# Set-up of an attention and mixture-of-experts kernel: keys in two halves, first maxima among other products, small loads on two other queues

## The reference

```python
q1 = split_heads(query @ q1_w.T); q2 = split_heads(query @ q2_w.T)      # query = layernorm(x)
k1, v1 = key @ kv1_w.T;           k2 = key @ kv2_w.T                    # key = context
attn1 = softmax(q1 k1^T * SCALE); attn2 = softmax(q2 k2^T * SCALE)
x = (attn1 - (lambda_1 - lambda_2 + 0.1) * attn2) @ v1
x = rmsnorm(x) * norm_w @ proj_w.T + proj_b                             # added to the input
probs = softmax(layernorm(x) @ gate_w.T); w, idx = top_k(probs, 2); w = w / sum(w)
out = x + sum over chosen experts of w_e * ((silu(x @ g_e.T) * (x @ u_e.T)) @ down_e.T)
```

## Time and profile before

| | us |
|---|---|
| median of 3 runs | 556.72 |
| lowest, highest run | 552.91, 558.14 |
| span of the profiled execution | 555.4 |
| PE busy, share | 495.3, 89% |
| DVE, ACT, POOL busy | 386.1, 340.2, 273.4 |

### The profile page before, as it was taken

How to read it: one execution, slowest core, us unless ns; L and a number is a source line. 1 busy time by engine, 2 the same in 40 slices (tenths; PEclk the granted TensorE clock), 3 DMA queues, 4 the chain that set the end, 5 groups by cost and what they waited for, 6 DMA issues and landing times.

```text
span 555.4 us, 12114 instructions
## 1 busy us (share of the span) xinstructions
PE 495.3 (89%) x3741; PEld 363.6 (65%) x3756; DVE 386.1 (70%) x805; ACT 340.2 (61%) x642; POOL 273.4 (49%) x347
## 2 busy tenths in 40 slices
PE   4695889998999888799798999999999999999990
PEld 3463546775666555526566888878888888777750
DVE  5437458888888765788577997887667677666551
ACT  1220588888788888374675777766656566645530
POOL 5006464574564564203227566656567555644244
PEclk9986799999999989899999999999999999999996
DMA  7567757768658632563666777967555465554224
GB/s 215 191 171 174 239 147 231 203 171 264 192 170 253 200 118 76 179 204 112 152 137 111 158 129 195 180 120 157 94 104 86 85 84 101 96 68 77 30 30 47
DMA packets 88090, 79.89 MB, mean 144 GB/s; under 512 B 49176, under 2 KB 73368, under 8 KB 87896
## 3 DMA queue, kind: packets, MB, share of 16 engines
q1 hardware_dynamic: 76512, 63.38, 41.8%
q0 software_dynamic: 11520, 15.74, 17.6%
HBM read 49.08 MB, written 22.41 MB: 129 GB/s over the span
## 4 chain that ended last, share of the span: by engine, by line
PE 67%; DVE 10%; ACT 7%; DMA 5%; issue 5%; SPq 3%; POOL 2%; another core or an unknown queue 0%; ACTq 0%; POOLq 0%
PE bank L1459 27%; PE bank L1476 13%; PE bank L1242 5%; PE bank L1288 4%; DMA x_parts<-WE 3%; PE bank L1274 3%; PE bank L1488 2%; PE bank L1256 2%; PE bank L1311 2%; PE bank L1324 2%; DVE FB L1165 2%; PE bank L1297 2%; DVE FB L1169 2%; ACT FB L876 2%; PE bank L1336 2%
## 5 line engine op out<-in xcount | busy, mean ns | idle before, releaser
L1459 PE MATMUL bank<-FB,WE 128*128 128x0 bf16 x1440 | 187.6, 280 | 2.6 <-issue 1.0
L1459 PEld LDWEIGHTS bank<-FB,WE 128*128 x1440 | 136.1, 98 | 34.9 <-issue 4.3
L709 POOL DMA_INDIRECT out<-FB,slot_tok x60 | 99.9, 1665 | 91.2 <-DVE FB L1186 85.4
L876 ACT ACTIVATE FB<-FB 128x512 bf16<-128x512 f32 x120 | 75.6, 630 | 69.9 <-DVE FB L1165 63.8
L1169 DVE TENSOR_TENSOR FB<-FB 128x512 bf16<-128x512 f32 x120 | 83.3, 694 | 46.9 <-ACT FB L876 43.0
L1476 PE MATMUL bank<-FB,WE 128*128 128x0 bf16 x720 | 103.7, 280 | 4.3 <-DVE FB L1169 2.2
L1165 DVE TENSOR_TENSOR FB<-FB,bank 128x512 f32<-128x512 f32 x120 | 81.9, 683 | 27.8 <-ACT FB L870 21.5
L700 POOL DMA_INDIRECT FB<-x_parts,slot_tok x60 | 61.7, 1028 | 68.0 <-DMA FB<-FB 26.7
L870 ACT ACTIVATE FB<-bank 128x512 f32<-128x512 f32 x120 | 70.7, 589 | 33.9 <-PE bank L1459 29.3
L1476 PEld LDWEIGHTS bank<-FB,WE 128*128 x720 | 67.6, 98 | 23.5 <-issue 7.8
L633 POOL TENSOR_TENSOR WE<-FB,WE 128x256 bf16<-128x256 f32 x104 | 67.8, 678 | 22.1 <-ACT WE L740 22.0
(11 more groups left out here) (180 smaller groups left out, 616.4 us busy)
## 6 DMA issues: line engine op xcount, KB each, us to landing
FB<-w SPq DMA_DIRECT2D x26, 512.0 KB, 5.5
WE<-w SPq DMA_DIRECT2D x44, 256.0 KB
WE<-q_parts SPq DMA_DIRECT2D x32, 200.0 KB
WE<-x SPq DMA_DIRECT2D x16, 256.0 KB, 5.2
q_parts<-FB SPq DMA_DIRECT2D x32, 128.0 KB
x_parts<-WE SPq DMA_DIRECT2D x20, 128.0 KB, 4.0
out<-WE SPq DMA_DIRECT2D x20, 128.0 KB, 5.5
q_parts<-WE SPq DMA_DIRECT2D x16, 128.0 KB
```

Source lines behind the costliest of these rows:

```text
L709: pool.indirect_dma_start(out=out, out_offset=bass.IndirectOffsetOnAxis(ap=slot_tok[:, c:c + 1].bitcast(U32), axis=0), in_=result_tile(c), ...
L876: nc.scalar.activation(hT[k % 3][:, 0, :], hid[k % 2], ACT.Copy).then_inc(hi_ready, 1)
L1459: ins = nc.tensor.matmul(to, wf[:, bass.ds(at + o, P)], xgT[s % 2][:, 2 * part + kc, :].shape_from_register(long[s % 2]), start=(z == 0), ...
```

## The change

It touches the set-up alone; the steps of the batches and the experts' stage stay as they are.

- Keys are made in two halves of four batches (308 columns each), in two sets of tiles and two tensors in device memory. The second half comes after the queries of batch 0. `scores` of batch 0 waits for all of it, `scores_for_max` only for the first.
- The 12 groups of scores for batch 0 start after two of the eight value products; the other six, the queries of batch 1 and the transposition of batch 2 stand between them.
- Queries of batch 2 come after the transposed maxima, the second half of them after the first two `scores`.
- Values are copied by ACT in place of DVE.
- ACT issues the reads of batch 0's keys (4 transfers in place of 8) behind a wait for `kd_out`, and the two `shifts` transfers of batch 0.
- Nine small loads (projection, gate, norm weights, bias, lambdas) go from SP's queue to POOL's. POOL's roots for batch 1 come before its four clears.
- x of batch 1 is loaded into `xd`, early; x of batch 2 follows at once.
- The high parts of pieces 2 and 3 (ACT) come after the first `exp`; the run-in of the tables is gone.

```diff
+        k_bank = [bank[0:4], [*bank[4:6], *bank[2:4]]]
...
-        for b in range(-4, B + 3):
+        for b in range(B + 3):
...
             for k in range(KC):
                 sp.dma_start(wq_sb[:, k, :], wqT[k * P:(k + 1) * P, :]).then_inc(wq_in, 16)
+            load_x(1)
             for k in range(KC):
                 sp.dma_start(wv_sb[:, k, :], wvT[k * P:(k + 1) * P, :]).then_inc(wv_in, 16)
-            for k in range(KC):
-                sp.dma_start(pj_sb[:, k, :], projT[k * P:(k + 1) * P, :]).then_inc(smalls_in, 16)
...
-            load_x(1)
...
+            load_x(2)
...
             pool.wait_ge(xn_ready, TPB)
+            for k in range(KC):
+                pool.dma_start(pj_sb[:, k, :], projT[k * P:(k + 1) * P, :]).then_inc(smalls_in, 16)
+                pool.dma_start(gate_sb[:, k, :], gateT[k * P:(k + 1) * P, :]).then_inc(smalls_in, 16)
+                pool.dma_start(normw[:, k:k + 1], norm_w[k * P:(k + 1) * P, :]).then_inc(smalls_in, 16)
+            pool.dma_start(bias_bc, proj_b.partition_broadcast(P)).then_inc(smalls_in, 16)
+            pool.dma_start(lams[:, 0, :], lam1.partition_broadcast(P)).then_inc(smalls_in, 16)
+            pool.dma_start(lams[:, 1, :], lam2.partition_broadcast(P)).then_inc(smalls_in, 16)
+            ln1(1)
             nc.gpsimd.memset(qst[1].rearrange("p h q -> p (h q)").bitcast(F32), 0.0).then_inc(stack1_ready, 1)
...
+            for m in range(4):
+                keys_hi(0, m)
             for a in range(2):
                 q_hi(0, a)
+            act.wait_ge(kd_out[0], 16 * 4)
+            act.wait_ge(stack0_ready, 3)
+            for a in range(2):
+                rows = slice(64 * a, 64 * a + 2 * HD), slice(64 * a + 2 * HD, 64 * a + 3 * HD)
+                for to, r in zip(rows, (2 * HD, HD)):
+                    act.dma_start(kst[0][to, :, a * SK:(a + 1) * SK], kd[0][a, 0:r, :, 0:SK]).then_inc(kst_in[0][0], 16)
+            for m in range(4):
+                keys_hi(1, m)
             xnT_copy(1)
+            values(0)
+            values(1)
...
+            mt_copy(0)
+            act.wait_ge(mT_ready, 1)
             for a in range(2):
+                act.dma_start(qst[0][64 * a + 48:64 * a + 50, :, :], mT[2 * H * a:2 * H * (a + 1), :]).then_inc(m_in, 16)
+            values(7)
+            q_hi(2, 0)
+            exp(0, 0)
+            q_hi(2, 1)
+            hi_part(2)
+            hi_part(3)
...
             q_lo(0, 0)
             q_lo(0, 1)
...
             ln1_norm(1)
+            for m in range(4):
+                keys_lo(1, m)
+            ln1_stats_of(2)
+            ln1_norm(2)
+            for g in range(4):
+                maxima(0, g)
             q_lo(1, 0)
...
+            keys(0)
+            queries(0, 0)
+            queries(0, 1)
+            keys(1)
+            transposed_x(1)
+            values(0)
+            values(1)
+            scores_for_max(0, 0)
+            scores_for_max(0, 1)
             queries(1, 0)
+            scores_for_max(0, 2)
+            scores_for_max(0, 3)
...
```

More of the change, by code:

```diff
@@ L219, in moe_attention_kernel @@
         qd = [nc.dram_tensor(f"q_parts{p}", [2, QROWS, H, S], BF16, kind="Internal").ap() for p in range(2)]
[L220 removed]
+        kd = [nc.dram_tensor(f"k_parts{n}", [2, 3 * HD, H, KW], BF16, kind="Internal").ap() for n in range(2)]
         xs = nc.dram_tensor("x_parts", [T + SUB * P, 2 * D], BF16, kind="Internal").ap()
@@ L234, in moe_attention_kernel @@
         kl_ready = sem("kl_ready")
-        kd_out = sem("kd_out")
+        kd_out = [sem(f"kd_out{n}") for n in range(2)]
+        kd_again = sem("kd_again")
         v_mm = sem("v_mm")
@@ L546, in _ @@
                 queries_lo_out(1, a)
-            sp.wait_ge(kd_out, 16 * 6)
+            sp.wait_ge(kd_out[0], 16 * 4)
+            sp.wait_ge(kd_again, 16 * 2)
             sp.wait_ge(stack1_ready, 3)
             for half in range(2):
-                queries_in(1, half)
+                keys_in(1, half)
             for n in range(STG, SPLIT_FIRST + STG):
                 load_piece(n)
+            for half in range(2):
+                queries_in(1, half)
             load_x(3)
@@ L984, in _ @@
             step(nc.vector.tensor_scalar(lams[:, 2, :], lams[:, 2, :], -0.1, None, ALU.add))
-            ln1_stats_of(2)
-            ln1_norm(2)
-            for g in range(12):
-                maxima(0, g)
+            ln1_stats_of(3)
+            q_lo(2, 0)
             for kind, i, b in steps(DVE_PLAN, DVE_END):
@@ L1338, in _ @@
                 ins.then_inc(v_mm, 1)
+            keys(0)
[7 more added lines that the diff above has]
+            scores_for_max(0, 1)
             queries(1, 0)
+            scores_for_max(0, 2)
+            scores_for_max(0, 3)
             queries(1, 1)
-            transposed_x(2)
+            scores_for_max(0, 4)
+            scores_for_max(0, 5)
+            values(2)
+            scores_for_max(0, 6)
+            scores_for_max(0, 7)
+            transposed_x(2)
+            values(3)
+            scores_for_max(0, 8)
+            scores_for_max(0, 9)
+            values(4)
+            scores_for_max(0, 10)
+            scores_for_max(0, 11)
+            values(5)
+            values(6)
+            transposed_max(0)
+            values(7)
+            queries(2, 0)
+            scores(0, 0)
+            scores(0, 1)
+            queries(2, 1)
+            scores_for_max(1, 0)
+            scores_for_max(1, 1)
             pe.wait_ge(pj_ready, 2)
             pe.wait_ge(smalls_in, 16 * 9)
-            for g in range(12):
-                scores_for_max(0, g)
             unit = [0]
```

165 lines of the change are left out of this document (89 added, 76 removed).

## The result

The change measured **556.17 us** (median of 20 runs, 548.71 to 559.78); the kernel before, run beside it, 558.31 (552.91 to 561.86). The ratio is 0.9927, 95% interval 0.9902 to 0.9952 (it leaves disturbed runs out of both sides, so it isn't the quotient of the medians). That is some 4 us gained, where 11.5 were forecast. The forecast was 545.2; the measured median lies outside the range of 539 to 553, and the ratio applied to 556.72 gives 552.7, at its upper edge.

The account below looks back on a forecast made before the run. PE was taken to bound the kernel, losing time to pauses and low clock in the set-up. First `scores` 17.6 us earlier, less 3.6, 2.0 and 0.3, gives 11.7, forecast as 11.5: 545.2 us from 556.72, range 539 to 553.

Parts of the forecast that it names:

- rival A: Set-up: POOL's queue is slow, nine loads take 18.8 us and delay batch 1's roots; gain 5.7, 551.0 us; chance 0.12.
- The rule of the Trainium skill: POOL's nine set-up loads: descriptor writes wait for a port DVE takes in some modes; would cost a few us, counted as nothing.
- added 2.4 for the clock: Stretch before batch 0's transposed maxima: one episode of PE's low clock costs 2.4 us, moving them from 39.6 to 42.
- If x of batch 1 is ready by 22.6: Set-up, value products: PE is through at 24.9 without the old pause of 4.20 us, if that x is ready.
- 3.6 us from the last query write: Batch 0's queries: reads go out 3.6 us after the last write's issue, at 23.9, giving first scores at 28.0.
- I take 4.5: Batch 0: 4.5 us from transposed maxima to `scores`, 3.9 before; first `scores` at 46.5 in place of 64.1.
- x of batch 3 and the eight clearing stores go out earlier by the same shift: SP's transfers at the end of the set-up: they move earlier with the first `scores`, at no cost in the sum.
- stand behind them and ahead of the second `exp`: ACT, batch 0: high parts, 1.04 us each, delay the second `exp`; fourth `scores` at 52.2, 3.6 us given back in all.
- So ACT waits 1.7: Batch 0: piece 4 lands at 58.7, ACT needs it at 57.0 and waits 1.7 us, the next `exp` and PE behind.
- 14.0 less 11.8: Fourth `scores` 14.0 us earlier, high part of piece 4 11.8 us earlier; the sum has 2.0 given back here.
- B: Rival: PE's clock stays low to the first `scores`, 8.4 us early, 3.6 given back; gain 4.5, 552.2 us; chance 0.13.
- E: Rival: an unseen wait in batch 0 or 1 takes back the gain at the first `scores`; 556 us; chance 0.04.

Follow-up runs that it names:

- the modified base: The change with SP's queue reordered by urgency (pieces 2 and 3, x of batch 3 earlier, clearing stores later) and 16-row key and query writes: 552.45 us, ratio 0.9894.

## Why the prediction was wrong

**Right:** keys, queries and keys again on PE (queries from 14.47 in one run of 3.62, second half to 22.2 against 22.6). POOL's nine loads: 0.54 to 0.81 each against the 1 us taken, roots of batch 1 done at 18.9 against 18.6. This takes rival A out:

```profile
6.88 0.81 POOL L679 DMA_DIRECT2D WE<-projT  x1 [0.77 <-DVE FB L974]
8.79 0.56 POOL L679 DMA_DIRECT2D WE<-projT  x1
17.18 0.18 POOL L665 TENSOR_SCALAR WE<-WE 128x1 f32<-128x1 f32 x1 [5.17 <-DVE WE L967]
```

The rule of the Trainium skill, SBUF — State Buffer, section "SBUF: two separate sides", that was weighed against it speaks of some modes of DVE. The trace does not name modes, so it neither bears the rule out nor refutes it. What it has is DVE clearing from 6.93 to 10.26 beside the first six issues: behind the first they took 0.54 to 0.59, like the two at which DVE was idle (0.55, 0.54).

**Luck:** the transposed maxima at 41.4 and 42.7 against 42. The forecast had the first score group at 28.0 and added 2.4 for the clock; the group came at 30.3, and the stretch ran at 1.00 in the first profile, so two errors of the same size cancelled. The low clock did come, but earlier (0.65 from 24.4 to 28.4), under the value products.

**"If x of batch 1 is ready by 22.6":** it was ready at 23.1. DVE's two normalizations took 3.75 us, where two of them elsewhere take 0.82; POOL's clears, which the change had put just there, ran beside them:

```profile
19.36 3.75 DVE L974 TENSOR_SCALAR FB<-WE 128x256 f32<-128x256 f32 x2
```

PE stood 0.94 for it and 1.89 a little later, where no pause was forecast before 24. Neither shows in the sum, since the reads of the first scores were later still.

**3.6 us from the last query write, "So the reads go out at 23.9":** mis-sized. Reads out at 26.11, 5.9 behind the last write's issue; the first score group 2.3 late. The mechanism was right. The value products, late themselves, ended at 29.3, so PE stood only 1.05 for it.

**From transposed maxima to `scores`, "I take 4.5":** the first step that failed. The row of 3.9 came from a stretch with a DMA share of 0.23. Moved 19 us forward, the rows met the reads of batch 1's queries, pieces, x and clearing stores, and the step took 7.0 and 11.7. That other work keeps its place behind them was assumed, and never priced.

**"x of batch 3 and the eight clearing stores go out earlier by the same shift":** costed at nothing, wrong. SP's queue was dense from 26.1 on, so x went out at 45.87, 5.6 earlier than before and not 17.6, and took 8.5, with DVE's reductions behind it: the fourth `scores` at 57.8 in place of 52.2.

**The high parts of pieces 2 and 3 "stand behind them and ahead of the second `exp`":** the step that failed most. ACT's 2.1 us were counted, the eight quarters on POOL behind them (5.1) and the roots of batch 3 between were not. I followed piece 2 through POOL to price piece 4's buffer and did not see that the roots are in that same queue. Undoing this alone gave 7.4 us on the modified base, and some 2 to 4 on the change (0.9891 against 0.9927, intervals overlapping, and 0.9970, intervals just apart).

**"So ACT waits 1.7" for piece 4:** it came without a wait at 63.64 in one profile, with 0.42 in the other; the chain was late elsewhere. Two small sums are off as well, without effect: 14.0 less 11.8 is 2.2, not 2.0, and B's gain by its own terms is 4.8, not 4.5.

Of the rivals, **E** (0.04) comes nearest: the gain at the first `scores` is taken back behind it, in part by transfers, in part by ACT's order, which is no transfer. It was given 0.04 because "every step of the tables counts from the step before"; but x and the reads are steps of a *queue*, and their time depends on what stands before them there. B's low clock came (0.67 from 48.4, 0.50 from 57.4) behind the pauses; the run that filled one of them got 2.0 us back in the trace.

## What to carry to other kernels

When a stage is pulled forward, price its transfers from rows in which the queues are as full as they will be, not from their old place; list all that is in flight in the new window, and put the smallest, most awaited transfer first. And follow each moved instruction through every engine behind it to the end of that queue: the place of two 1 us instructions on ACT was worth up to 7 us, since POOL, DVE and PE stood behind them in turn.

## What the runs showed of the hardware

- 32 KB in 68 packets (two DMAs on ACT's queue) landed 2.3 us after the last issue began with SP's queue nearly empty (8.9% of the engines' time from 45 to 47), and 9.6 after it beside a full one (97% from 50 to 52).
- SP's issues themselves stretch: the same four reads of keys took SP 1.9 to 2.2 us in ten traces (all eight with sixteen-row writes, two with eight rows), and 3.0 to 4.0 in seven, all with eight rows. What sets it is not shown.
- Two executions of the change differ by 6 us at the first `scores` (48.4 and 54.4), and 7 in the whole span; 1.3 of the 6 stand there at the transposed maxima, the rest is the landing of the rows.
- DVE's two normalizations of batch 1 took 2.0 to 4.3 us in all 17 traces in which POOL's clears ran beside them (in the change one took 2.52 in place of 0.41, the clears ran from 18.9 to 24.2), and 0.82 where none did. No run takes the clears away, so the cause is not shown.
